# A layer norm's first half is moved from the openings of three attentions into the tails of the feed-forwards before them

## The chip, the cores and the metric

One NeuronCore of a Trainium2 chip runs the whole program in one launch. The metric is the device time of an execution in microseconds. A core has five engines that run their own instruction queues in order and meet by semaphores: TensorE (PE in the profile), VectorE (DVE), ScalarE (ACT), GpSimd (POOL) and SyncE (SP), which here only issues transfers.

## The reference

Four layers, each an attention and a feed-forward, on x of 8 batches x 100 tokens x 512 features, in float32. The context has 8 x 361 tokens.

```python
x = x + _L0_xattn_ref(_layernorm(x, axis=-1), ctx_2048, itok_BxS_0_1023, ...)
x = x + _L0_ffn_ref(_layernorm(x, axis=-1), ...)
x = x + _L1_xattn_ref(_layernorm(x, axis=-1), ctx_2048, mask_BxS2_ik0, ...)
x = x + _L1_ffn_ref(_layernorm(x, axis=-1), ...)
x = x + _L2_xattn_ref(_layernorm(x, axis=-1), ctx_2048, ...)
x = x + _L2_ffn_ref(_layernorm(x, axis=-1), ...)
x = x + _L3_xattn_ref(_layernorm(x, axis=-1), ctx_2048, ctx_2048, mask_BxS2_ff1, ...)
x = x + _L3_ffn_ref(_layernorm(x, axis=-1), ...)

def _layernorm(x, axis=-1, eps=1e-05):
    m = jnp.mean(x, axis=axis, keepdims=True)
    v = jnp.var(x, axis=axis, keepdims=True)
    return (x - m) / jnp.sqrt(v + eps)
```

Attentions 1, 2 and 3 project the normed x to queries and the context to keys and values, with 16 heads of 32. Feed-forward 0 adds to a shared network two of eight experts for each token; feed-forward 1 rounds activations and weights to few levels; feed-forward 2 is a gated network with 2048 inner features; feed-forward 3 sends each of 512 tokens to four of 16 experts.

## The kernel before, in words

**Layout.** The residual lies in SBUF feature-major: 128 partitions, KD = 4 tiles of features, T = 800 tokens in two halves of HALF = 400 (four batches of S = 100). float32 products are made of three products of rounded parts: a high part, copied by ScalarE, and a low part, what is left, subtracted by VectorE or GpSimd (`product`, L101 to L109).

**Stages.** Eight stages run one after the other: `l0x`, `l0f` (RoutedFfn), `l1x` (BoundedAttention), `l1f` (BitFfn), `l2x` (Attention), `l2f` (Ffn), `l3x` (LinearAttention), `l3f` (ChosenFfn). Each has a method for each engine, and the order of an engine's work is the order in which the code is written. Nothing is planned at run time. A stage ends when VectorE has made its last residual add and raises `residual_ready`; the next stage's GpSimd, SyncE and ScalarE work waits for it. VectorE and TensorE need no such wait for work on the first half of the tokens, because the adds of the first half are made first.

**The norm** (`Norm`) of a stage works by batches b of 100 tokens. `turn` transposes a batch on TensorE into a PSUM bank (16 transposes for four batches, L139). `stats` and `moments` on VectorE give mean and variance (L145, L151), `deviation` on ScalarE the square root (L156, which needs the table with Sqrt), `inverse` on VectorE the reciprocal and the shift (L162, L164), `normalise` on ScalarE the normed rows (L173), `back` on TensorE turns them back (L180), `high` on ScalarE (L186) and `low` on VectorE (L192) make the two parts. Deviation and inverse work on pairs of batches, so VectorE and ScalarE wait for each other twice in a half. The second half's turns use the banks of the first half, and each waits for the low part of the batch four earlier (`half_turn`).

**An opening** is what attentions 1, 2 and 3 do until their batches run (`Attention.pe`, `act`, `dve`, `pool`). ScalarE copies the high part of the context (L1810) and of twelve weight slabs (L1775), GpSimd subtracts the low parts (L1802, L1770), TensorE makes four key products (`pe_keys`), each of which needs one weight, then three value products (`pe_values`), which need eight weights, and then the query projection, which needs the norm and twelve weights. ScalarE copies the keys' high part (L1852), VectorE makes their low part (L1858). In the kernel before, the first half's statistics and normalising are in the opening, between the context copy and the weight copies, and the half turn of the second half stands between the second and the third key product. The slabs 6 to 11 are loaded into the buffers of slabs 0 to 5 when those are split.

**A tail** is a feed-forward's last product and its residual adds. The half turn of the next norm's first half already stands in the tails. In `l0f`, two expert sums come from DRAM in two transfers, one for each half (`sum_landed0`, `sum_landed1`); VectorE adds the two experts (`sums`, L1200), TensorE transposes them (`pe_sum`, L935), VectorE adds them to the residual (`add`, L1194). In `l1f` the last batch goes from the product (L2846) over ScalarE's copy (L2906) and four transposes (L2865) to the add (L2978). In `l2f` the last product is made in eight units of half the tokens, in four banks, each with an add (L683).

## Time and profile before

| | |
|---|---|
| Median of 3 runs | 2395.26 us (2393.09 to 2398.01) |
| Profiled execution | 2396.35 us, its span 2394.5 us |
| TensorE matmul busy | 2101.5 us, 88% |
| VectorE busy | 1086.1 us, 45% |
| ScalarE busy | 911.3 us, 38% |
| GpSimd busy | 495.7 us, 21% |
| Chain that ended last | TensorE 65%, DMA 11%, VectorE 10%, ScalarE 7%, issue 5% |

Times in the profile are microseconds from the start of the span. In the timeline a row is one instruction or several alike: start, duration, engine, line, operation, output and inputs; in brackets the idle time of its engine before it and what ended it. The granted clock is a share of TensorE's full clock of 2.4 GHz; 0.50 is 1.2 GHz. In the trace l1x opens at about 760 us, l2x at 1203 and l3x at 1776.

### The profile page before, as it was taken

The page shows a single profiled execution, that of the slowest core. Times are in us where ns is not written, and L with a number is a line of the kernel's source. Part 1 is how long each engine was busy: PE and PEld are TensorE (multiplying, and loading weights), DVE is VectorE, ACT ScalarE, POOL GpSimd, SP SyncE. Part 2 cuts the span into 40 slices and gives each one's busy share as a digit, 9 for nine tenths or more (in the row PEclk, how much of TensorE's full clock was granted, in tenths as well). Part 3 has the DMA queues.
Part 4 walks back from the last instruction along what each step waited for, and adds up shares of the span by engine and source line. Part 5 has one row for each costly group of instructions (what it writes and reads, how often), then busy time and mean ns, then how long its engine had stood idle before and what let it go on. Part 6 is the DMA issues. An engine that isn't in the chain of part 4 may idle for free.

```text
span 2394.5 us, 39229 instructions
## 1 busy us (share of the span) xinstructions
PE 2101.5 (88%) x14719; PEld 1693.1 (71%) x14719; DVE 1086.1 (45%) x2401; ACT 911.3 (38%) x1738; POOL 495.7 (21%) x358
## 2 busy tenths in 40 slices
PE   6989999896996888987978999889987999979997
PEld 5976666686445777775566777789986999945554
DVE  4447667565114255558825666422332555511111
ACT  3346556433222344455645454332233322222221
POOL 2233232232231211100031110033322111013322
PEclk7889999998997899978989999899999999989998
DMA  3110010127224121122020000021121100379995
GB/s 107 58 39 26 13 38 1 54 66 278 74 84 129 43 88 45 49 86 111 20 65 23 26 25 2 27 75 57 45 75 43 35 25 13 110 244 311 324 317 152
DMA packets 90860, 203.68 MB, mean 85 GB/s; under 512 B 9198, under 2 KB 14418, under 8 KB 88594
## 3 DMA queue, kind: packets, MB, share of 16 engines
q1 hardware_dynamic: 80562, 174.82, 22.4%
q0 software_dynamic: 10144, 26.75, 4.2%
q8 instruction: 104, 1.70, 0.3%
q14 instruction: 50, 0.41, 0.1%
HBM read 183.84 MB, written 19.53 MB: 85 GB/s over the span
## 4 chain that ended last, share of the span: by engine, by line
PE 65%; DMA 11%; DVE 10%; ACT 7%; issue 5%; POOL 1%; SPq 1%; ACTq 0%; DVEq 0%; POOLq 0%
PE psum L106 15%; PE psum L107 13%; PE psum L109 13%; DMA l3f_sum_dram<-l3f_y,l3f_rows 8%; PE psum L887 3%; PE psum L3376 2%; PE psum L2608 2%; PE psum L3346 2%; PE psum L2068 1%; PE psum L913 1%; PE psum L2273 1%; PE psum L1528 1%; DVE l2x_highest L2150 1%; PE psum L3362 1%; DVE ln_stats L145 1%
## 5 line engine op out<-in xcount | busy, mean ns | idle before, releaser
L1528 PE MATMUL psum<-l3f_gate_up,l3f_x_turned 128*128 128x352 f32 x496 | 154.2, 464 | 0.8 <-ACT l3f_x_turned L1587 0.8
L1528 PEld LDWEIGHTS psum<-l3f_gate_up,l3f_x_turned 128*128 128x128 f32 x496 | 93.0, 193 | 48.1 <-issue 1.7
L3135 POOL TENSOR_TENSOR l0x_w_lo<-l0x_w_raw,l0x_w_hi 128x512 fp32r<-128x512 f32 x52 | 71.8, 1398 | 152.0 <-ACT l0x_w_hi L3388 127.5
L2109 ACT ACTIVATE l2x_probs<-psum,l2x_shift 100x361 f32<-100x361 f32 x128 | 65.0, 559 | 98.2 <-DVE l2x_shift L2154 97.0
L3490 ACT ACTIVATE l0x_probs<-l0x_probs,l0x_lowest 100x361 f32<-100x361 f32 x128 | 75.1, 588 | 59.8 <-DVE l0x_lowest L3654 59.6
L106 PE MATMUL psum<-xn_hi,l2f_w_gu_hi 128*128 128x400 f32 x256 | 89.7, 350 | 8.8 <-ACT l2f_silu L588 4.9
L1802 POOL TENSOR_TENSOR l2x_ctx_lo<-l2x_ctx_raw,l2x_ctx_hi 128x1448 fp32r<-128x1448 f32 x8 | 26.3, 3289 | 339.8 <-ACT l2x_ctx_hi L1810 339.7
L107 PE MATMUL psum<-xn_lo,l2f_w_gu_hi 128*128 128x400 f32 x256 | 88.8, 347 | 0.0
L1503 POOL DMA_INDIRECT l3f_sum_dram<-l3f_y,l3f_rows x31 | 49.2, 1587 | 183.3 <-DMA l3f_sum_dram<-l3f_y,l3f_rows 143.6
L1554 PE MATMUL psum<-l3f_down,l3f_h_turned 128*128 128x512 f32 x186 | 85.1, 593 | 0.9 <-DVE l3f_h_turned L1619 0.9
L443 POOL TENSOR_TENSOR l2f_w_gu_lo<-l2f_raw_gu,l2f_w_gu_hi 128x512 fp32r<-128x512 f32 x32 | 43.0, 1353 | 203.6 <-ACT l2f_w_gu_hi L458 203.6
L1613 DVE TENSOR_TENSOR l3f_h<-l3f_silu,psum 128x352 f32<-128x352 f32 x31 | 16.2, 521 | 151.7 <-ACT l3f_silu L1600 120.4
L2302 ACT ACTIVATE ln_squares<-l1x_clipped,l1x_key_shift,l1x_key_scale 128x400 f32<-128x400 f32 (+1 forms) x96 | 62.3, 712 | 54.1 <-DVE l1x_clipped L2332 54.1
L887 PE MATMUL psum<-l0f_weights,l0f_x_turned 128*128 x160 | 75.2, 614 | 1.2 <-ACT l0f_x_turned L1029 0.8
L3376 PE MATMUL psum<-ln_squares,l0x_l_turned 128*128 128x400 f32 (+1 forms) x192 | 73.1, 516 | 0.9 <-ACT ln_squares L3499 0.9
L3654 DVE CUSTOM_DVE_ANT_0 l0x_probs<-psum,l0x_outside 100x361 f32<-100x361 f32 x128 | 62.6, 529 | 24.0 <-PE psum L3346 21.7
L641 DVE TENSOR_TENSOR l2f_h<-l2f_silu,psum 128x800 f32<-128x800 f32 x16 | 15.8, 988 | 125.7 <-PE psum L109 116.2
L3362 PEld LDWEIGHTS psum<-identity,l0x_probs 100*128 100x128 f32 (+1 forms) x384 | 38.0, 153 | 44.8 <-DVE l0x_probs L3665 20.3
L109 PE MATMUL psum<-xn_hi,l2f_w_gu_lo 128*128 128x400 f32 x256 | 69.3, 347 | 0.0
L2642 ACT ACTIVATE ln_squares<-psum 64x64 f32<-64x64 f32 x128 | 28.0, 218 | 105.9 <-PE psum L2608 103.5
L106 PE MATMUL psum<-l1x_w_hi,l1x_ctx_hi 128*128 128x512 f32 (+1 forms) x96 | 45.5, 474 | 25.5 <-DVE l1x_k_lo L1858 17.9
L3362 PE MATMUL psum<-identity,l0x_probs 100*128 100x100 f32 (+1 forms) x384 | 50.1, 265 | 19.9 <-DVE l0x_probs L3665 12.8
(533 smaller groups left out, 6181.1 us busy)
## 6 DMA issues: line engine op xcount, KB each, us to landing
l3f_gate_up<-in_slabs_dram SPq DMA_DIRECT2D x31, 1280.0 KB, 7.8
l3f_down<-in_slabs_dram SPq DMA_DIRECT2D x31, 512.0 KB
l0x_w_raw<-in_slabs_dram SPq DMA_DIRECT2D x52, 256.0 KB, 2.8
l0f_weights<-in_slabs_dram SPq DMA_DIRECT2D x8, 1536.0 KB
l1x_piece<-in_bit_w_dram SPq DMA_DIRECT2D x8, 1024.0 KB, 4.8
l1f_raw<-in_bit_w_dram SPq DMA_DIRECT2D x8, 1024.0 KB, 9.0
l2f_raw_gu<-in_slabs_dram SPq DMA_DIRECT2D x32, 256.0 KB, 2.6
l3f_down<-in_slabs_dram SPq DMA_DIRECT2D x31, 192.0 KB
```

Source lines behind the costliest of these rows:

```text
L106: pe.matmul(outs[i], weight_hi, moving[i][0], start=first, stop=False)
L107: pe.matmul(outs[i], weight_hi, moving[i][1], start=False, stop=False)
L109: mm = pe.matmul(outs[i], weight_lo, moving[i][0], start=False, stop=last)
L887: mm = pe.matmul(c.psum[:, t % 2, :], self.x_turned[:, t % 2, k, :], self.weights[:, bass.DynSlice(expert, 1), k * 512:(k + 1) * 512].rear ...
L1528: mm = pe.matmul(c.psum[:, bank + x, 0:self.INNER], self.x_turned[:, t % 2, k, :], self.gate_up[:, q, at:at + self.INNER], start=k == 0, s ...
L1554: mm = pe.matmul(c.psum[:, 6 + t % 2, :], self.h_turned[0:z - a, t % 2, k, :], self.down[0:z - a, q, k, :], start=k == 0, stop=k == 2)
L2109: act.activation(self.probs[:, m % 2, g, :], c.psum[0:S, g, 0:C], ACT.Exp, bias=self.shift[:, g:g + 1], scale=self.SCALE).then_inc(self.s( ...
L3135: pool.tensor_tensor(self.w_lo[:, place, :], self.w_raw[:, n % 3, :], self.w_hi[:, place, :], ALU.subtract).then_inc(self.s("w_split"), 1)
L3362: mm = pe.transpose(c.psum[0:z - a, 4 + t, g * S:(g + 1) * S], self.probs[:, g, a:z], c.identity[0:S, 0:S])
L3376: mm = pe.matmul(c.psum[:, 6, 0:4 * S], self.l_turned[0:z - a, q, t, :], turned[0:z - a, t, :], start=t == 0, stop=t == 2)
L3490: act.activation(self.probs[:, g, :], self.probs[:, g, :], ACT.Exp, bias=self.lowest[:, g:g + 1], scale=-1.0, accum_out=self.total[:, g:g ...
L3654: dve.tensor_tensor_reduce(self.probs[:, g, :], c.psum[0:S, g, 0:C], self.outside[:, q, :], -self.SCALE, 3.0e38, ALU.add, ALU.min, self.lo ...
```

## The change

In the tails of feed-forwards 0, 1 and 2, VectorE now also makes the first half's statistics, inverse and shift (`half_dve(..., 0)`), and ScalarE its deviation and normalised rows (`rows_ahead`, in `l1f` `half_rows`). In `l0f` the half turn moves from behind two of the second half's four sums to in front of them, and VectorE makes the first half's four adds and the statistics before it adds the experts of the second half. In `l2f` the half turn moves one unit forward and the statistics stand behind the fifth add. In `l1f` they stand in front of the last batch's add. The attentions open with the four turns back of the first half, then the turns of the second half, and then the key products; ScalarE makes the four high parts first, then weight copies and the second half's norm.

```diff
+def rows_ahead(n, act):
+
+    n.root_table(act)
+    half_rows(n, act, 0)
...
@@ ffn_pe, down: last product of l2f
-                if u == KD + 2:
+                if u == KD + 1:
                     pe.wait_ge(c.sem(st.name + "_added"), chunk * KD + KD)
                     half_turn(c.norms[st.index + 1], pe, 0)
@@ ffn_act
     ffn_schedule(act, st, gate_up, down)
+    rows_ahead(c.norms[st.index + 1], act)
@@ ffn_dve, down: adds of the last product
+                if u == KD:
+                    half_dve(c.norms[st.index + 1], dve, 0)
@@ RoutedFfn.pe
         for u in range(2 * KD):
-            if u == KD + 2:
+            if u == KD:
                 pe.wait_ge(self.s("added"), 3 * KD)
                 half_turn(c.norms[self.index + 1], pe, 0)
             self.pe_sum(c, pe, u)
@@ RoutedFfn.act
         out(self.TILES - 1)
+        rows_ahead(c.norms[self.index + 1], act)
@@ RoutedFfn.dve
         for u in range(KD):
             add(u, 2 * KD + u)
-            if u == 0:
-                sums(1)
+        half_dve(c.norms[self.index + 1], dve, 0)
+        sums(1)
         for u in range(KD, 2 * KD):
             add(u, 2 * KD + u)
@@ Attention.pe
-        n.back(pe, 0)
-        n.back(pe, 1)
-        self.pe_keys(pe, 0, 0, 0)
-        n.back(pe, 2)
-        n.back(pe, 3)
-        self.pe_keys(pe, 0, 0, 1)
+        half_back(n, pe, 0)
         pe.wait_ge(c.sem("residual_ready"), self.index + 1)
         half_turn(n, pe, 1)
-        self.pe_keys(pe, 0, 0, 2)
+        self.pe_keys(pe, 0, 0, 0)
+        self.pe_keys(pe, 0, 0, 1)
         n.back(pe, 4)
         n.back(pe, 5)
+        self.pe_keys(pe, 0, 0, 2)
         self.pe_keys(pe, 0, 0, 3)
         n.back(pe, 6)
         n.back(pe, 7)
@@ Attention.act
         self.split_context_high(act, 0, 0)
-        self.split_weight_high(act, 0)
-        n.deviation(act, 0)
-        n.normalise(act, 0)
-        n.normalise(act, 1)
-        n.deviation(act, 1)
-        self.split_weight_high(act, 1)
-        n.high(act, 0)
-        n.high(act, 1)
-        n.normalise(act, 2)
-        n.normalise(act, 3)
-        self.split_weight_high(act, 2)
-        n.high(act, 2)
-        n.high(act, 3)
+        for b in range(4):
+            n.high(act, b)
+        for i in range(2):
+            self.split_weight_high(act, i)
+        for g in (2, 3):
+            n.deviation(act, g)
+            n.normalise(act, 2 * g)
+            n.normalise(act, 2 * g + 1)
+            self.split_weight_high(act, g)
         act.wait_ge(self.s("vectors_landed"), 16)
         self.act_keys(act, 0, 0, 0)
-        self.split_weight_high(act, 3)
-        n.deviation(act, 2)
-        n.normalise(act, 4)
-        n.normalise(act, 5)
-        n.deviation(act, 3)
+        self.split_weight_high(act, 4)
         self.act_keys(act, 0, 0, 1)
         n.high(act, 4)
         n.high(act, 5)
-        n.normalise(act, 6)
-        n.normalise(act, 7)
-        self.split_weight_high(act, 4)
+        self.act_keys(act, 0, 0, 2)
         n.high(act, 6)
         n.high(act, 7)
-        self.act_keys(act, 0, 0, 2)
         self.act_keys(act, 0, 0, 3)
         for i in range(5, 12):
             self.split_weight_high(act, i)
@@ Attention.dve
-        half_dve(n, dve, 0)
         half_low(n, dve, 0)
+        half_dve(n, dve, 1)
...
         self.dve_keys(dve, 0, 0, 0)
-        half_dve(n, dve, 1)
         self.dve_keys(dve, 0, 0, 1)
-        half_low(n, dve, 1)
+        n.low(dve, 4)
+        n.low(dve, 5)
         self.dve_keys(dve, 0, 0, 2)
+        n.low(dve, 6)
+        n.low(dve, 7)
         self.dve_keys(dve, 0, 0, 3)
@@ BitFfn.act
         self.schedule(act, first, body)
+        half_rows(c.norms[self.index + 1], act, 0)
@@ BitFfn.dve
         self.schedule(dve, first, body)
+        half_dve(c.norms[self.index + 1], dve, 0)
         add(B - 1)
```

## Rows read from the trace of the kernel before

**Rows 1.** Timeline, opening of attention 1: start us, us, engine line
```profile
760.50 1.41 ACT L1810 ACTIVATE l1x_ctx_hi<-l1x_ctx_raw 128x1448 fp32r<-128x1448 f32 x1 [34.81 <-DVEq L1211]
...
762.06 3.23 POOL L1802 TENSOR_TENSOR l1x_ctx_lo<-l1x_ctx_raw,l1x_ctx_hi 128x1448 fp32r<-128x1448 f32 x1 [35.13 <-ACT l1x_ctx_hi L1810]
...
764.27 1.04 DVE L164 SCALAR_TENSOR_TENSOR ln_shift<-ln_moments,ln_inverse 100x2 f32<-100x2 f32 x1
...
771.40 0.90 ACT L186 ACTIVATE xn_hi<-psum 128x400 fp32r<-128x400 f32 x2 [1.14 <-PE psum L180]
...
771.94 1.06 DVE L192 TENSOR_TENSOR xn_lo<-psum,xn_hi 128x400 fp32r<-128x400 f32 x2 [2.88 <-ACT xn_hi L186]
...
773.55 1.91 PE L139 MATMUL psum<-identity,residual 128*100 128x128 f32 x16
...
774.19 1.29 DVE L145 BATCH_NORM_STATS2 ln_stats<-psum 100x6 f32<-100x512 f32 x2 [0.69 <-PE psum L139]
...
776.98 0.16 DVE L164 SCALAR_TENSOR_TENSOR ln_shift<-ln_moments,ln_inverse 100x2 f32<-100x2 f32 x1
...
777.26 1.45 ACT L173 ACTIVATE ln_squares<-psum,ln_shift,ln_inverse 100x512 f32<-100x512 f32 x2 [1.23 <-DVE ln_shift L164]
...
779.10 0.41 PE L106 MATMUL psum<-l1x_ctx_hi,l1x_w_hi 128*128 128x362 f32 x1
...
779.12 0.16 DVE L164 SCALAR_TENSOR_TENSOR ln_shift<-ln_moments,ln_inverse 100x2 f32<-100x2 f32 x1
...
781.17 0.92 PE L180 MATMUL psum<-identity,ln_squares 100*128 100x100 f32 x8
...
782.62 1.07 ACT L1852 ACTIVATE l1x_k_hi<-psum,l1x_vectors 128x362 fp32r<-128x362 f32 x2
...
783.51 3.29 ACT L1775 ACTIVATE l1x_w_hi<-l1x_w_raw 128x512 fp32r<-128x512 f32 x6
...
784.28 8.68 POOL L1770 TENSOR_TENSOR l1x_w_lo<-l1x_w_raw,l1x_w_hi 128x512 fp32r<-128x512 f32 x7 [0.95 <-ACT l1x_w_hi L1775]
...
788.15 0.77 PE L106 MATMUL psum<-l1x_w_hi,l1x_ctx_hi 128*128 128x512 f32 x1 [6.06 <-POOL l1x_w_lo L1770]
```

**Rows 2.** Timeline, openings of attentions 2 and 3: first context copy, first value product
```profile
1202.61 1.41 ACT L1810 ACTIVATE l2x_ctx_hi<-l2x_ctx_raw 128x1448 fp32r<-128x1448 f32 x1 [1.32 <-DVEq L2999]
...
1230.99 0.77 PE L106 MATMUL psum<-l2x_w_hi,l2x_ctx_hi 128*128 128x512 f32 x1 [6.05 <-POOL l2x_w_lo L1770]
...
1776.01 1.41 ACT L1810 ACTIVATE l3x_ctx_hi<-l3x_ctx_raw 128x1448 fp32r<-128x1448 f32 x1 [11.93 <-DVEq L697]
...
1804.41 0.77 PE L106 MATMUL psum<-l3x_w_hi,l3x_ctx_hi 128*128 128x512 f32 x1 [6.05 <-POOL l3x_w_lo L1770]
```

**Rows 3.** Timeline, tail of feed-forward 0
```profile
742.88 2.59 PE L935 MATMUL psum<-identity,l0f_weights 100*128 100x100 f32 x14 [0.48 <-DVE l0f_weights L1200]
...
743.51 0.57 DVE L1194 TENSOR_TENSOR residual<-residual,psum 128x400 f32<-128x400 f32 x1 [0.69 <-PE psum L935]
...
750.95 2.36 DVE L1200 TENSOR_TENSOR l0f_weights<-l0f_weights 100x1024 f32<-100x1024 f32 x2 [6.87 <-DMA l0f_weights<-l0f_y_dram]
...
754.81 3.65 PE L139 MATMUL psum<-identity,residual 128*100 128x128 f32 x16 [0.18 <-DVE residual L1194]
```

**Rows 4.** Stretch 766 to 774 us: busy us by engine; PEclk, DMA share, GB/s last
```profile
766.00:774.00 8.00, 7.74 (x45) 7.63 (x46) 2.94 (x7) 6.13 (x13) 3.72 (x4) 0.73 0.32 100
```

**Rows 5.** Timeline, tail of feed-forward 1
```profile
1200.61 0.69 ACT L2906 ACTIVATE l1f_out<-psum,l1f_h_step 100x512 f32<-100x512 f32 x1 [4.60 <-PE psum L2846]
...
1201.95 0.57 DVE L2978 TENSOR_TENSOR residual<-residual,psum 128x400 f32<-128x400 f32 x1 [5.97 <-PE psum L2865]
```

**Rows 6.** Timeline, tail of feed-forward 2
```profile
1771.22 1.91 PE L139 MATMUL psum<-identity,residual 128*100 128x128 f32 x16
...
1775.35 0.57 DVE L683 TENSOR_TENSOR residual<-residual,psum 128x400 f32<-128x400 f32 x1 [0.52 <-PE psum L109]
```

**Rows 7.** DMA issues from 724 to 800 us: KB each, median us to landing
```profile
l1x_w_raw<-in_slabs_dram SPq DMA_DIRECT2D x12, 256.0 KB, 8.1
```

## The prediction

> **What bounds the kernel now.** I read the chain of work that ended last first, then the timeline around the three places where a feed-forward hands over to an attention. In all three the same thing ends last. The attention's opening is a relay: ScalarE makes the high part of the context (L1810), norms and weights follow, TensorE makes the four key products, and then it stands idle for 6.06 us until GpSimd has split the eighth weight (L1770), which the value products need [rows 1]. I measure an opening from A, the start of L1810, which starts right behind the residual's last add, to V, the start of the first value product. It takes 788.15 - 760.50 = 27.65 us in the first attention [rows 1], and 28.38 and 28.40 us in the others [rows 2]. After V the products run on, and the weights that the projection needs are split some 8 us ahead of it, so what moves V moves the end. The reader is to see that V hangs on a row of queues: the fifth to eighth weights go to GpSimd only behind ScalarE's last key copy, and this copy stands behind the last two norm turns (781.17) and their high parts [rows 1].
>
> **The openings: the new V.** The first half's statistics and normalising leave the opening. What is left, counted from A = 0 with the durations of [rows 1]:
> - Context copy 1.41, four high parts at 0.45 each: 3.2. Two weight copies at 0.55: 4.3.
> - VectorE's lows start at 2.0 behind the first high; four at 0.53 end at 4.1. TensorE's turns of the second half start behind the first low, at 2.6. The first is read long before 4.1 at either clock.
> - Statistics start at 4.15. From there to the end of the first shift it takes 777.14 - 774.19 = 2.95: 7.1. Two normalisings 1.45: 8.65. The third weight copy, 0.6: 9.25. Deviation, inverse and shift of the last pair ended 0.57 behind the normalising in front of them (778.71 to 779.28); behind a weight copy I take 0.7: 9.95.
> - Here a block: L164 (two small inputs in SBUF) normally takes 0.16, but 1.04 at 764.27, and it ended at 765.31, within 0.02 us of the end of GpSimd's 3.23 us split that had begun at 762.06 [rows 1]. The new shift falls on the third weight's split (9.3 to 10.6), so I end it at 10.65.
> - Two normalisings: 12.15; the fourth weight copy: 12.75; its split on GpSimd, 1.24 (8.68 for 7): 14.05. The fourth key product may start at 14.1.
> - TensorE itself: four turns at the lower clock, 3.65 as in [rows 3], end at 6.2. The granted clock rose inside the stretch after the first turns, with a mean of 0.73 over 8 us, so about 4.3 us of it at 1.2 GHz and the rest at 2.4 [rows 4]. So the first key product, 2.07 at full clock (779.10 to 781.17), costs some 0.7 more and ends at 9.0; the second 11.1, two norm turns 0.92: 12.0, the third 14.1. It meets the weight at the same time.
> - Fourth key product to 16.2, where the last two norm turns start. From there to V it took 788.15 - 781.17 = 6.98 in the kernel before, with two key copies in it (1.07); now the third key is copied earlier, so 6.5: V = 22.7.
> The gains are 27.65 - 22.7 = 4.95, 5.7 and 5.7: 16.35 us. The bounds: without the block and with TensorE at full clock from the turns on, it is free at 13.1 and the weight is there at 13.4, so V = 22.0 (-2.1 in all); with each queue a further 0.7 late, +2.1. The table load in the first and third opening moves to the tail, where ScalarE has nothing else to do, and costs nothing; if that cover were gone it would stand once before the tail's first deviation.
>
> The Trainium skill, "SBUF — State Buffer", section "Who interferes with whom", states that a VectorE instruction with two SBUF inputs and a GpSimd instruction that reads SBUF exclude each other, and that the second to issue fully blocks until the first ends. The row agrees (1.04 against 0.16 us). By that rule the sum holds the block, as above; without it V could be up to 0.7 us earlier in each opening, if TensorE is also ready. The low parts (L192) have one input in PSUM, and by the same rule they don't wait; 1.06 us for two beside a GpSimd split agrees.
>
> **The tails: what is added there.** Statistics, deviation, inverse, shift of the first half stand now in VectorE's queue in front of the last residual adds. Each pair makes VectorE wait for ScalarE, and queued behind that wait are the adds, for which the whole next stage waits.
> - Feed-forward 0. In the kernel before, TensorE's half turn (3.65) stands between the sums of the last two-expert transfer and A [rows 3]. Adds 1 to 3 stood behind that transfer (750.95); now they run beside TensorE's 14 transposes (742.88, 2.59), the last to 746.25, and the half turn runs in the DMA's wait, to 749.95. The statistics follow the turns; the fourth ends at 750.75, inverse 751.1, two normalisings to 752.65, deviation and second shift 753.25. So the sums start at 753.3, not at 750.95: 2.35 late. From their end to A it took 760.50 - 753.31 = 7.2, less the turn 3.54. A = 753.3 + 2.36 + 3.54 = 759.2: 1.3 us earlier. If the turns ran at full clock, the sums would start at 752.1: 2.5 earlier.
> - Feed-forward 1. ScalarE's last output copy ends at 1201.30 [rows 5]. Then deviation 0.3, inverse and shift 0.4, two normalisings 1.45, deviation and shift 0.7 (less overlap): second shift at 1204.15, the last add (0.57) behind it, end 1204.8 instead of 1202.5. ScalarE then still has two normalisings, 1204.3 to 1205.7, ahead of L1810. A moves from 1202.61 to 1205.65: 3.05 later. Here nothing covers the wait, since ScalarE is late itself.
> - Feed-forward 2. The half turn starts one unit (1.1) earlier, at 1770.1 instead of 1771.22 [rows 6]; the fifth add ends at 1770.9; the whole statistics sequence of two pairs takes 779.28 - 774.19 = 5.09 [rows 1]: 1776.0. Adds 5 to 7, 0.58 each, end at 1777.8, against 1775.92: 1.9 later, and A with them (it stood 0.09 behind that add, 1776.01). The products are done at the same time as before and wait in their banks.
> The four turns back of the first half are issued ahead of the residual wait and end about 2.4 us behind it at the low clock, before the third high part asks for them: no cost.
>
> **The sum.** -16.35 - 1.3 + 3.05 + 1.9 = -12.7 us. The profiled execution took 2396.35 us (span 2394.5 and 1.85 around it), 1.09 above the median of 2395.26; it would become 2383.65, and the median 2382.6. No transfer is added or passed on another queue.
>
> **Rivals.**
> - A, the slabs come late. V needs the weights 6 and 7, whose transfers are issued when weights 0 and 1 are split (A + 6.1 and 7.4). The median landing in this stretch is 8.1 us [rows 7], so 15.5, and ScalarE asks at 18 to 19. It speaks against this rival; from a landing of 11.5 us on it sets V. If it took the 15.6 us that eat up 4.2 an opening, the time stays at about 2395. A gate of another kind that leaves V at A + 26 to 27 belongs here too. Chance 0.08.
> - B, the tails cost more: the handshakes of two engines in three queues each 2 us longer than counted (the sums in feed-forward 0 then start at 755.3). Time 2388.6. Chance 0.09.
> - C, the tails cost nothing, because the adds or the turns overlap more than the queues say: -16.35 alone gives about 2379, with the full-clock bound 2377. Chance 0.07.
> - D, slower: TensorE stays at 1.2 GHz through the key products. The openings' turns now stand apart from the products, with waits on each low part. At the low clock a turn takes 3.65 against 1.91 [rows 1, 3], a factor 1.9: products of 3.9 and norm turns of 1.75 put the fourth key product at 6.2 + 3 x 3.9 + 1.75 = 19.7, the last norm turns at 23.6 and V at 30.9, 2.5 to 3.3 later than before. With the tails' 3.65 that is +12, 2407. It decides from 4.2 us per opening on. Against it: the clock rose here after some 4.3 us with the same sparse work in front [rows 4], and the products that follow are as dense. Chance 0.05.
>
> **How the numbers follow.** The forecast holds 0.71: 2382.6, its own range 2379 to 2387 from the bounds above (openings -2.1 and +2.1, tails -1.2 and +1.5, and 1 us of scatter). A 0.08, B 0.09, C 0.07, D 0.05. The range to 2378 and 2389 takes in B and most of C, and leaves A and D out. No change means within 0.2%, 4.8 us, about what a measurement of this kernel can tell. Faster: forecast, B, C: 0.87. Same: A, 0.08. Slower: D, 0.05.
>
> **What would show it.** In the profile of the changed kernel: the idle of TensorE before the first value product still stands at 5 to 6 us, but V - A is 22 to 23.5 in all three; a shift of about 0.8 to 1 us ending with a GpSimd split, at A + 10; the half turn of feed-forward 0 between 746 and 750; its sums not at the DMA's landing but 2 us behind; the last add of feed-forward 1 behind a second shift, with two normalisings behind it. The forecast is wrong if V - A stays above 25, if a table load shows between the last deviation and the context copy, or if an add waits for ScalarE more than 5 us.

## The result and the profile after

The changed kernel took 2381.39 us (median of 4 runs, 2380.65 to 2383.91) against 2394.77 us for the kernel before (4 runs, 2393.09 to 2398.01). The ratio is 0.9942, with a 95% interval of 0.9927 to 0.9958: 13.4 us faster, where 12.7 was forecast. A second series gave 2380.40 us (median of 6 runs) against 2395.01 (e1 below).

A and V are again the starts of ScalarE's first context copy (now L1820) and of the first value product. The timeline of the changed kernel, opening of attention 1, answers to [rows 1]; the first column is the start, the second the duration:

```profile
757.50 1.41 ACT L1820 ACTIVATE l1x_ctx_hi<-l1x_ctx_raw 128x1448 fp32r<-128x1448 f32 x1 [4.05 <-DVEq L1221]
...
760.05 3.62 PE L139 MATMUL psum<-identity,residual 128*100 128x128 f32 x16 [0.59 <-DVE xn_lo L192]
...
766.97 1.29 POOL L1780 TENSOR_TENSOR l1x_w_lo<-l1x_w_raw,l1x_w_hi 128x512 fp32r<-128x512 f32 x1 [2.18 <-ACT l1x_w_hi L1785]
767.31 0.97 DVE L164 SCALAR_TENSOR_TENSOR ln_shift<-ln_moments,ln_inverse 100x2 f32<-100x2 f32 x1
...
771.79 0.43 PE L106 MATMUL psum<-l1x_ctx_hi,l1x_w_hi 128*128 128x362 f32 x1 [1.15 <-POOL l1x_w_lo L1780]
...
773.88 0.85 PE L180 MATMUL psum<-identity,ln_squares 100*128 100x100 f32 x8
...
775.21 0.57 ACT L1862 ACTIVATE l1x_k_hi<-psum,l1x_vectors 128x362 fp32r<-128x362 f32 x1
775.66 3.23 ACT L1785 ACTIVATE l1x_w_hi<-l1x_w_raw 128x512 fp32r<-128x512 f32 x6
776.38 4.95 POOL L1780 TENSOR_TENSOR l1x_w_lo<-l1x_w_raw,l1x_w_hi 128x512 fp32r<-128x512 f32 x4 [3.39 <-ACT l1x_w_hi L1785]
780.24 0.77 PE L106 MATMUL psum<-l1x_w_hi,l1x_ctx_hi 128*128 128x512 f32 x1 [5.50 <-POOL l1x_w_lo L1780]
```

The last row is V. TensorE still stands idle in front of it (5.50 us, 6.06 before), and it still waits for GpSimd's split of the eighth weight, but V - A is 22.74. The other two openings answer to [rows 2]:

```profile
1199.06 1.41 ACT L1820 ACTIVATE l2x_ctx_hi<-l2x_ctx_raw 128x1448 fp32r<-128x1448 f32 x1
...
1221.81 0.76 PE L106 MATMUL psum<-l2x_w_hi,l2x_ctx_hi 128*128 128x512 f32 x1 [5.50 <-POOL l2x_w_lo L1780]
...
1769.98 1.41 ACT L1820 ACTIVATE l3x_ctx_hi<-l3x_ctx_raw 128x1448 fp32r<-128x1448 f32 x1
...
1792.71 0.77 PE L106 MATMUL psum<-l3x_w_hi,l3x_ctx_hi 128*128 128x512 f32 x1 [5.50 <-POOL l3x_w_lo L1780]
```

That is 22.75 and 22.73. The three gains are 4.91, 5.63 and 5.67, together 16.21 us (16.35 forecast).

The timeline of the changed kernel in the tail of feed-forward 0, for [rows 3]:

```profile
739.41 2.36 DVE L1210 TENSOR_TENSOR l0f_weights<-l0f_weights 100x1024 f32<-100x1024 f32 x2 [7.19 <-DMA l0f_weights<-l0f_y_dram]
...
745.08 3.65 PE L139 MATMUL psum<-identity,residual 128*100 128x128 f32 x16 [0.66 <-DVE residual L1204]
...
751.72 0.16 DVE L164 SCALAR_TENSOR_TENSOR ln_shift<-ln_moments,ln_inverse 100x2 f32<-100x2 f32 x1
751.79 2.35 DVE L1210 TENSOR_TENSOR l0f_weights<-l0f_weights 100x1024 f32<-100x1024 f32 x2
```

The last sums stand right behind the second shift and no longer wait for the DMA. From the first sums to A it takes 757.50 - 739.41 = 18.09 us, against 760.50 - 740.47 = 20.03 before: 1.94 less.

The tail of feed-forward 1, for [rows 5]:

```profile
1194.19 0.69 ACT L2904 ACTIVATE l1f_out<-psum,l1f_h_step 100x512 f32<-100x512 f32 x1 [4.60 <-PE psum L2844]
1194.78 0.28 ACT L156 ACTIVATE ln_std<-ln_moments,eps 100x2 f32<-100x2 f32 x1
...
1197.52 0.56 DVE L2977 TENSOR_TENSOR residual<-residual,psum 128x400 f32<-128x400 f32 x1
1197.72 1.45 ACT L173 ACTIVATE ln_squares<-psum,ln_shift,ln_inverse 100x512 f32<-100x512 f32 x2 [0.51 <-DVE ln_shift L164]
```

A (1199.06) stands 4.87 us behind the start of the output copy, against 2.00 before: 2.87 more. And the tail of feed-forward 2, for [rows 6], with ScalarE's table load at its head:

```profile
1756.63 1.28 ACT L201 ACT_TABLE_LOAD   x1
...
1758.57 0.57 DVE L690 TENSOR_TENSOR residual<-residual,psum 128x400 f32<-128x400 f32 x1 [1.59 <-PE psum L109]
...
1768.36 1.52 DVE L690 TENSOR_TENSOR residual<-residual,psum 128x400 f32<-128x400 f32 x3
1768.57 1.45 ACT L173 ACTIVATE ln_squares<-psum,ln_shift,ln_inverse 100x512 f32<-100x512 f32 x2 [0.51 <-DVE ln_shift L164]
```

From the first unit's add to A it takes 1769.98 - 1758.57 = 11.41 us, against 9.99: 1.42 more. The table load and the small instruction behind it are followed by 6.8 us of idle time on ScalarE.

The account of the two spans (2394.5 and 2382.1, -12.4): openings -16.21; tails -1.94, +2.87 and +1.42; ahead of the first tail -1.06; the three stretches behind V +1.49, +1.73 and -0.70. So the openings and tails gave -13.86, where -12.7 was forecast, and the rest +1.46, where nothing was.

### The profile page after: what moved, and what is told of

The parts are those of the page before. It is cut to its first block, busy times and chain, and to the rows that moved or that the text cites. A ratio compares the mean times of both kernels' runs of the same rounds, so it can differ in the third digit from the quotient of the medians.

```text
span 2382.1 us, 39231 instructions
## 1 busy us (share of the span) xinstructions
PE 2103.5 (88%) x14719; PEld 1692.8 (71%) x14719; DVE 1085.5 (46%) x2401; ACT 912.1 (38%) x1740; POOL 496.0 (21%) x358
## 4 chain that ended last, share of the span: by engine, by line
PE 65%; DMA 11%; DVE 10%; ACT 7%; issue 5%; POOL 1%; ACTq 0%; SPq 0%; DVEq 0%; POOLq 0%
PE psum L106 15%; PE psum L107 13%; PE psum L109 13%; DMA l3f_sum_dram<-l3f_y,l3f_rows 9%; PE psum L896 3%; PE psum L3376 2%; PE psum L2606 2%; PE psum L3346 2%; PE psum L2066 2%; PE psum L922 1%; PE psum L2271 1%; DVE l2x_highest L2148 1%; PE psum L3362 1%; PE psum L2621 1%; DVE ln_stats L145 1%
## 5 line engine op out<-in xcount | busy, mean ns | idle before, releaser
L106 PE MATMUL psum<-l1x_w_hi,l1x_ctx_hi 128*128 128x512 f32 (+1 forms) x96 | 46.2, 481 | 25.1 <-DVE l1x_k_lo L1868 18.1
L3362 PE MATMUL psum<-identity,l0x_probs 100*128 100x100 f32 (+1 forms) x384 | 50.1, 265 | 19.9 <-DVE l0x_probs L3665 12.8
```

What stands on the lines that cost most here:

```text
L106: pe.matmul(outs[i], weight_hi, moving[i][0], start=first, stop=False)
L3362: mm = pe.transpose(c.psum[0:z - a, 4 + t, g * S:(g + 1) * S], self.probs[:, g, a:z], c.identity[0:S, 0:S])
```

## The experiments

All runs stand beside runs of the kernel before on the same chip, at 2394.2 to 2395.0 us in the median, and each ratio below is to these, with its 95% interval. Each kernel is the changed kernel with the edit shown. One table for all: V - A of the three openings; "path", the sum of the stretches that the change touches (first sums to A, output copy to A, first unit's add to A, and three times from A to VectorE's first value add, here W, which reads the first value product); the path against the changed kernel's; the median; and the median against 2381.39. The last column compares medians of different series, and the runs of one kernel lie 3 to 12 us apart, so one or two microseconds in it show nothing. The path is read from one profiled execution of each kernel.

| kernel | V - A | path | path, difference | median us | difference |
|---|---|---|---|---|---|
| before | 27.65, 28.38, 28.40 | 131.26 | +12.9 | 2394.77 | +13.4 |
| changed | 22.74, 22.75, 22.73 | 118.41 | 0 | 2381.39 | 0 |
| e1 | 22.74, 22.76, 22.74 | 118.23 | -0.2 | 2380.40 | -1.0 |
| e2 | 19.35, 19.37, 19.34 | 103.10 | -15.3 | 2364.89 | -16.5 |
| e3 | 21.45, 22.30, 21.44 | 113.84 | -4.6 | 2376.78 | -4.6 |
| e4 | 22.73, 22.72, 23.00 | 117.23 | -1.2 | 2382.66 | +1.3 |
| e5 | 22.74, 22.75, 22.74 | 120.37 | +2.0 | 2384.84 | +3.5 |
| e6 | 22.74, 22.70, 22.74 | 123.00 | +4.6 | 2384.80 | +3.4 |
| e7 | 29.73, 29.72, 29.74 | 136.37 | +18.0 | 2398.77 | +17.4 |
| e8 | 18.07, 18.64, 18.04 | 99.65 | -18.8 | 2361.29 | -20.1 |
| e9 | 22.73, 22.73, 22.72 | 115.43 | -3.0 | 2377.94 | -3.5 |
| e10 | 18.05, 18.07, 18.49 | 95.68 | -22.7 | 2359.26 | -22.1 |
| e11 | 16.41, 16.41, 16.41 | 88.99 | -29.4 | 2356.28 | -25.1 |

**e1, the changed kernel again, unedited.**

> The changed kernel itself once more, to see what repeats. If the working by queues holds, V - A (start of the context copy to the first value product) repeats at 22.7 us in all three openings, and the time is 12.5 to 13.5 us below the kernel before. The stretches between the openings, which the change does not touch, differed by +1.5, +1.7 and -0.7 us between the two profiles: if that is scatter of the clock's phase, they come out otherwise here, by 1 us or so either way; if the change costs something there, +1.5 and +1.7 repeat.

Ratio 0.995, interval 0.9934 to 0.9966: 14.6 us below the kernel before (12.5 to 13.5 expected). V - A and the tails repeat within 0.03 us, A to W within 0.2. The first stretch behind V took 410.17 us, not 413.95, at a higher granted clock (PEclk, third from the end; the changed kernel, then e1):

```profile
780.24:1194.19 413.95, 357.66 (x4062) 284.80 (x4062) 244.90 (x570) 206.99 (x306) 33.10 (x15) 0.89 0.17 62
778.95:1189.10 410.15, 353.52 (x4062) 281.64 (x4062) 245.05 (x570) 206.92 (x306) 33.10 (x15) 0.90 0.17 63
```

The other two did not come out otherwise: 536.73 and 589.40 us, against 536.76 and 589.39 in the changed kernel and 535.03 and 590.11 before. By the test set above, the first stretch's +1.49 was scatter, while the second's +1.7 speaks for a cost of the change there; 0.85 of it is the first value product alone (5.50 us against 4.65 before). But in e5, whose openings are the same, this product took 4.35 and the stretch 533.52, so the cause stays open.

**e2, is V set by when ScalarE hands over the weights?**

```
         self.act_keys(act, 0, 0, 1)
+        self.split_weight_high(act, 5)
         n.high(act, 4)
         n.high(act, 5)
+        self.split_weight_high(act, 6)
         self.act_keys(act, 0, 0, 2)
+        self.split_weight_high(act, 7)
...
-        for i in range(5, 12):
+        for i in range(8, 12):
```

> ScalarE copies weights 5, 6 and 7 between the key copies and the high parts, no longer behind the last key copy. Theory (V hangs on ScalarE's and GpSimd's queues): GpSimd works through the weights 3 to 7 with hardly a gap, the eighth is split at A + 19.3 instead of 22.7, so V - A is 19.4 in each opening, 3.4 less; TensorE idles 2 us instead of 5.5, and if it then keeps its full clock, the first value product group costs up to 2 us less. In all 10 to 16 us below the changed kernel: 2365 to 2371. Rival (the transfers of slabs 6 and 7 set V): V - A stays at 22.7, time within 2 us of the changed kernel, and ScalarE waits on the transfer in front of the seventh copy.

Ratio 0.9874 (0.9859 to 0.9888), V - A 3.4 us less in each opening. Timeline of this kernel (its A is 758.04), and then the windows (engine busy times, PEclk third from the end) from V to W, of the changed kernel and of this one, in opening 2:

```profile
771.00 11.20 POOL L1780 TENSOR_TENSOR l1x_w_lo<-l1x_w_raw,l1x_w_hi 128x512 fp32r<-128x512 f32 x9 [2.20 <-ACT l1x_w_hi L1785]
...
777.39 0.76 PE L106 MATMUL psum<-l1x_w_hi,l1x_ctx_hi 128*128 128x512 f32 x1 [2.12 <-POOL l1x_w_lo L1780]
```

```profile
1221.81:1227.30 5.49, 5.46 (x12) 3.77 (x12) 0.00 (x0) 2.04 (x2) 5.41 (x5) 0.50 0.51 197
```

```profile
1211.73:1214.80 3.07, 3.04 (x12) 2.14 (x12) 0.00 (x0) 1.62 (x4) 3.07 (x3) 1.00 0.99 388
```

GpSimd now splits nine weights in a row from A + 12.96; the fifth of them is the eighth weight, and 12.96 + 5 x 1.24 = 19.2 is V. So from that split on GpSimd alone sets V. And the gain is larger than 3 x 3.4 = 10.2, because in openings 2 and 3 the first value product itself became shorter: in opening 2 5.49 us at a granted clock of 0.50 in the changed kernel, behind 5.50 us of idle, and 3.07 at 1.00 here, behind about 2 us. The prediction had counted only to V. The sum to W holds it (5.2 us in all). In opening 1 nearly nothing of this came, though the idle time in front was the same 2.12 us:

```profile
777.39:781.94 4.55, 4.50 (x12) 3.25 (x12) 0.01 (x1) 2.58 (x4) 4.55 (x4) 0.65 0.68 264
```

**e3, the shift out of the way of the third split.**

```
-        for g in (2, 3):
-            n.deviation(act, g)
-            n.normalise(act, 2 * g)
-            n.normalise(act, 2 * g + 1)
-            self.split_weight_high(act, g)
+        n.deviation(act, 2)
+        n.normalise(act, 4)
+        n.normalise(act, 5)
+        n.deviation(act, 3)
+        self.split_weight_high(act, 2)
+        n.normalise(act, 6)
+        n.normalise(act, 7)
+        self.split_weight_high(act, 3)
```

> The last pair's deviation is taken ahead of the third weight's copy, so its shift runs before GpSimd splits that weight. Theory (the shift is blocked by the split it overlaps): the shift takes 0.16 instead of 0.97 us, the fourth weight is split 1.3 us earlier, and V - A is 1.15 less where TensorE waited for it (openings 1 and 3 in the profile) and 0 in opening 2, where TensorE was busy: 2.3 us faster in all, 2379. Rival (0.97 is the operation's own time there, and nothing is blocked): the shift still takes 0.97, the weight comes 0.5 earlier, 1 us in all.

Ratio 0.9936 (0.9922 to 0.9949); V - A 1.29, 0.45 and 1.29 less. Timeline of this kernel:

```profile
765.48 0.16 DVE L164 SCALAR_TENSOR_TENSOR ln_shift<-ln_moments,ln_inverse 100x2 f32<-100x2 f32 x1
...
765.84 1.28 POOL L1780 TENSOR_TENSOR l1x_w_lo<-l1x_w_raw,l1x_w_hi 128x512 fp32r<-128x512 f32 x1 [2.36 <-ACT l1x_w_hi L1785]
```

The same instruction takes 0.16 us ahead of the split and 0.97 beside it. The shift ends at A + 9.45 instead of 10.78, and 0.81 of these 1.33 us is the block; the other 0.52 comes from the deviation's place ahead of the weight copy. Opening 2 was to gain nothing, because TensorE is busy there, and gained 0.45: its clock stood at 0.50 until A + 8.4, and the fourth key product began at A + 13.96, behind TensorE's own work, against 13.08 in opening 1. The expectation was 2.3 us in all; the path is 4.6 shorter, of which 3.0 lie in V - A, 1.3 in the first value products and 0.3 in the first tail.

**e4, feed-forward 0: sums ahead of the second inverse.**

```
         sums(1)
+        then.inverse(dve, 1)
```

(The rest of the first half's work stands in front of the sums as before.)

> In feed-forward 0 VectorE adds the experts of the second half before it makes the second pair's inverse and shift, so it no longer waits for ScalarE's normalising with the landed transfer behind it. Theory (this handshake holds the sums back by 1.9 us): from the first sums to A it takes 16.2 us instead of 18.1, time 1.9 below the changed kernel, 2379.5. Rival (the transfer lands only then): no change of A, and VectorE idle in front of the sums, released by the DMA.

The sums start again at the landing, 11.04 us behind the first sums instead of 12.38, and A comes 1.34 earlier (16.75), not the 1.9 expected, because VectorE now waits for the transfer:

```profile
749.51 2.36 DVE L1210 TENSOR_TENSOR l0f_weights<-l0f_weights 100x1024 f32<-100x1024 f32 x2 [0.56 <-DMA l0f_weights<-l0f_y_dram]
```

The median (ratio 0.9947, 0.9934 to 0.996) doesn't show so little; the stretch does.

**e5, feed-forward 1: the add ahead of the statistics.**

```
-        half_dve(c.norms[self.index + 1], dve, 0)
         add(B - 1)
+        half_dve(c.norms[self.index + 1], dve, 0)
```

> The changed kernel, but in the tail of feed-forward 1 VectorE makes the last residual add first and the first half's statistics, inverses and shifts behind it. It asks which queue sets A in this tail. Theory (ScalarE's: the context copy stands behind four normalisings, and these hang on VectorE's shifts): the add can start 1.34 us behind the output copy's start and ends at 1.9, so the first inverse starts at 1.9 instead of 0.9 and all behind it is 1.0 later: A stands 5.9 us behind the output copy instead of 4.87, and the time is 2382, 1 us above the changed kernel's. Rival (the last add sets A, as the prediction's working on feed-forward 2 has it): A stands 2.0 to 2.9 us behind the copy, and the time is 2378 to 2379.

The rival falls, and the expected number too: output copy (1190.61) to A is 8.37 us, not 5.9. Timeline of this kernel:

```profile
1191.95 0.57 DVE L2977 TENSOR_TENSOR residual<-residual,psum 128x400 f32<-128x400 f32 x1 [5.97 <-PE psum L2863]
1192.44 1.29 DVE L145 BATCH_NORM_STATS2 ln_stats<-psum 100x6 f32<-100x512 f32 x2
...
1198.98 1.41 ACT L1820 ACTIVATE l2x_ctx_hi<-l2x_ctx_raw 128x1448 fp32r<-128x1448 f32 x1
```

The residual is complete at 1192.5, and A comes 6.5 later. In this kernel VectorE raises the residual's signal only behind the statistics, so the distance alone doesn't tell which queue sets A; the changed kernel does. There the last add ends at 1198.08, and A comes 0.98 later without idle time behind ScalarE's last normalising. The expectation had counted only the inverses as moved behind the add; the edit moves the statistics too, which had run under the last products and now wait through 5.97 us for the add. Ratio 0.9958 (0.9942 to 0.9974).

**e6, feed-forward 0: the half turn back behind the DMA's wait.**

```
-            if u == KD:
+            if u == KD + 2:
...
-        half_dve(c.norms[self.index + 1], dve, 0)
-        sums(1)
+            if u == 0:
+                sums(1)
         for u in range(KD, 2 * KD):
             add(u, 2 * KD + u)
+            if u == KD + 1:
+                half_dve(c.norms[self.index + 1], dve, 0)
```

> The changed kernel, but in the tail of feed-forward 0 TensorE's half turn goes back behind the sixth sum and the statistics behind the sixth add, so that the sums of the last two-expert transfer again start at its landing; deviation, inverse, shift and normalising stay in the tail. It asks what the tail's earlier turn is worth. Theory (the turn in the DMA's wait pays for the pairs that VectorE now waits for): the stretch from the first sums to A is the 20.03 us of before plus about 2.3 for the statistics, the two pairs' turns between VectorE and ScalarE and the last adds behind them, so 22.3 against 18.09, and the time is about 4.3 us above the changed kernel's 2381: 2385. Rival (the last adds and the pairs overlap, so that the place of the turn doesn't matter): 18 to 19 us, and 2381 to 2382.

First sums to A is 22.64 us, 4.55 more; the time is 3.4 more (ratio 0.9958, 0.9943 to 0.9973). The half turn starts behind the sixth add, at 753.71, not inside the wait:

```profile
753.71 3.65 PE L139 MATMUL psum<-identity,residual 128*100 128x128 f32 x16 [0.18 <-DVE residual L1204]
```

So without the earlier turn this tail would have cost 2.6 us instead of giving 1.9.

**e7, the new order without the move.** The tails are those of the kernel before; in the opening:

```
         self.split_context_high(act, 0, 0)
+        half_rows(n, act, 0)
...
+        half_dve(n, dve, 0)
         half_low(n, dve, 0)
```

> The changed kernel's new order of the attention's opening (turns, then key products), but with no work in the tails: all three tails are those of before, and the statistics, deviations and normalisings of the first half stand at the head of the opening, behind the context copy. It tells the order's part from the move's. Theory (the openings are short because the first half's relay is gone, and the order only spends that): the relay of two pairs takes 5.1 to 6 us and lies again in front of the first high part, so V - A is 28.5 to 30 in all three; with 2.4 us less in the tails than in the changed kernel the time is 2396 to 2401, no better than before. Rival (the order alone brings the gain, because the weights are copied earlier): V - A is 23 to 26 and the time 2380 to 2390.

Ratio 1.0021 (1.0012 to 1.003): the order alone is some 4.6 us slower than the kernel before (2394.18 in this series). The timeline of its first opening:

```profile
759.97 1.28 ACT L156 ACT_TABLE_LOAD   x1
...
760.10 3.23 POOL L1808 TENSOR_TENSOR l1x_ctx_lo<-l1x_ctx_raw,l1x_ctx_hi 128x1448 fp32r<-128x1448 f32 x1 [36.11 <-ACT l1x_ctx_hi L1816]
...
761.79 1.56 DVE L164 SCALAR_TENSOR_TENSOR ln_shift<-ln_moments,ln_inverse 100x2 f32<-100x2 f32 x1
```

The relay's first shift is held up by the context's split and ends with it, at 763.35 and 763.33. V - A is 29.73, 29.72 and 29.74; the table load in the first lies under that split and adds nothing.

**e8, the three orders of e2, e3 and e4 together.**

> The changed kernel with three orders tried singly: weights 6 to 8 copied by ScalarE between the key copies, the last deviation ahead of the third weight copy, and in feed-forward 0 the last sums ahead of the second inverse and shift. Theory (what ends last in front of the value products is now GpSimd, which splits nine weights without a pause from A + 12.96 on, and value products need the fifth of them; the shift's order lets the fourth split start at A + 11.64 instead): V is 11.64 + 5 x 1.244 = 17.9, so V - A about 18.0 against 19.35 with the weights alone, 4 us less in three openings; the first sums to A take 16.75; time 2365 - 4 - 1.3 = 2359.5. Rival (TensorE's key products or the landing of the weights' transfers set V from here on): V - A stays at 19 or more, and the time is 2362 or more.

Ratio 0.9872 (0.9858 to 0.9886). The timeline, with A at 755.71:

```profile
767.37 11.21 POOL L1788 TENSOR_TENSOR l1x_w_lo<-l1x_w_raw,l1x_w_hi 128x512 fp32r<-128x512 f32 x9 [0.69 <-ACT l1x_w_hi L1793]
...
773.78 0.47 PE L106 MATMUL psum<-l1x_w_hi,l1x_ctx_hi 128*128 128x512 f32 x1 [2.11 <-POOL l1x_w_lo L1788]
```

11.66 + 5 x 1.245 = 17.9, and V follows at 18.07: GpSimd sets V, as expected, in openings 1 and 3. In opening 2 (18.64) the rival holds in part. TensorE's clock stood at 0.50 until A + 8.4, the fourth key product began at A + 13.95 instead of 13.12, and what ended last was VectorE's low part of the fourth key:

```profile
1208.77 0.80 PE L106 MATMUL psum<-l2x_w_hi,l2x_ctx_hi 128*128 128x512 f32 x1 [1.84 <-DVE l2x_k_lo L1876]
```

**e9, feed-forward 1: the first pair ahead of the output copy.**

```
+            if not now:
+                then.deviation(act, 0)
+                then.normalise(act, 0)
+                then.normalise(act, 1)
+                then.deviation(act, 1)
             if before:
...
-        half_rows(c.norms[self.index + 1], act, 0)
+        then.normalise(act, 2)
+        then.normalise(act, 3)
```

> The changed kernel, but in the tail of feed-forward 1 ScalarE makes the first deviation, the first pair of normalisings and the second deviation ahead of its last output copy, not behind it. Theory (the tail of feed-forward 1 costs 2.9 us because ScalarE takes up the first deviation only behind the output copy, although its statistics were there 3.8 us earlier and ScalarE stood idle for 4.6 us): the output copy starts 0.25 later at most, A stands about 2.1 us behind it instead of 4.87, so A is 2.5 us earlier, counted from TensorE's half turn of this tail (7.8 instead of 10.27), and the time is 2378.4. Rival (VectorE's last add or the landing of the products is what ends last): A moves by less than 1 us, and the time is 2380 to 2381.

Ratio 0.9938 (0.9925 to 0.9951). Timeline of this kernel:

```profile
1188.77 0.29 ACT L156 ACTIVATE ln_std<-ln_moments,eps 100x2 f32<-100x2 f32 x1 [1.43 <-DVE ln_moments L151]
...
1191.94 0.69 ACT L2911 ACTIVATE l1f_out<-psum,l1f_h_step 100x512 f32<-100x512 f32 x1
...
1193.94 1.41 ACT L1820 ACTIVATE l2x_ctx_hi<-l2x_ctx_raw 128x1448 fp32r<-128x1448 f32 x1
```

The copy to A is 2.00 us again, as in the kernel before, and the copy itself starts no later: from TensorE's half turn of this tail to A it is 7.40 us, against 10.28 in the changed kernel. So the whole cost of this tail, 2.87 us, was the place of four instructions in ScalarE's queue.

**e10, all four orders.**

> The three orders of the combined kernel, and the first pair of rows ahead of the last output copy in feed-forward 1. Theory (the parts lie in different stretches and add up): V - A about 18.1, 18.6 and 18.0, A 2.0 us behind the output copy in feed-forward 1, 16.7 us from the first sums to A; the time is the combined kernel's 2361.3 less 2.6 to 2.9: 2358.5. Rival (the time saved in one place is lost again behind it, as a later start of the second attention's weights): 2361 or more.

Ratio 0.9841 (0.9823 to 0.9858). The parts add up within 1 us: the path is 22.7 us shorter, against 18.8 for e8 and 3.0 for e9. The opening at 18.5 is here the third, again one whose clock was low into the first key products (to A + 8.1).

**e11, e10 with every weight early and the last key ahead of the last high parts.**

```
         n.deviation(act, 2)
+        self.split_weight_high(act, 2)
+        self.split_weight_high(act, 3)
         n.normalise(act, 4)
         n.normalise(act, 5)
         n.deviation(act, 3)
+        self.split_weight_high(act, 4)
...
         self.act_keys(act, 0, 0, 2)
+        self.act_keys(act, 0, 0, 3)
         n.high(act, 6)
         n.high(act, 7)
```

(Weights 5 to 7, counted from 0, follow behind key copies 0, 1 and high part 5; VectorE's low part of the last key moves in the same way.)

> The kernel with all four orders, and in the opening also: ScalarE copies the third and fourth weight behind the first two and the fifth behind the last deviation, so that GpSimd splits without a pause from the context's split on; and the last key product is copied ahead of the last two high parts. Theory (in the combined kernel V waits for two things that end together at A + 17.8, GpSimd's split of the eighth weight and VectorE's low part of the last key; TensorE itself is done at A + 16.0; GpSimd with 8 splits of 1.25 from A + 4.8 is done at 14.8): TensorE sets V, V - A is 16.3 to 16.9, and the time is some 4.5 us below the kernel with the four orders: about 2354. Rival (GpSimd without a pause holds up each shift until its split ends, up to 1.25 us each, as a two-input instruction of VectorE was held up before; or the slabs of the seventh and eighth weight land too late): the last pair of rows and with it the last norm turns come later, V - A stays at 17.5 or more, the time at 2357 or more.

Timeline of this kernel (A at 758.29), and the window from V to W:

```profile
763.08 6.25 POOL L1788 TENSOR_TENSOR l1x_w_lo<-l1x_w_raw,l1x_w_hi 128x512 fp32r<-128x512 f32 x5
...
767.59 0.52 DVE L164 SCALAR_TENSOR_TENSOR ln_shift<-ln_moments,ln_inverse 100x2 f32<-100x2 f32 x1
...
774.70 0.50 PE L106 MATMUL psum<-l1x_w_hi,l1x_ctx_hi 128*128 128x512 f32 x1 [0.60 <-DVE l1x_k_lo L1876]
```

```profile
774.70:777.80 3.10, 3.06 (x12) 2.17 (x12) 0.91 (x3) 2.98 (x6) 2.39 (x2) 1.00 0.90 341
```

V - A is 16.41 in all three. TensorE's idle in front of V is down from 5.50 to 0.60, and VectorE's low part of a key, which follows TensorE's last key product, releases it, no longer GpSimd. The shifts are still held up (0.52 ends at 768.11, with a split at 768.08), but those waits are covered by the key products. The time is 2356.28 us (2354 expected), ratio 0.9837 (0.9821 to 0.9854). Its path is 6.7 us shorter than e10's, the medians differ by 3.0, and the intervals overlap: what became of the rest is open.

## Why the prediction was right

- **Openings, right.** V hangs on the queues of ScalarE and GpSimd. e2 shows it by moving three weight copies and nothing else (V - A 3.4 less), and e8 by putting V where GpSimd's queue, counted out, has it in two openings; e7 shows that the relay of the first half (7.0 us of V - A) is what the move takes out, and that the new order without it is slower.
- **Inside the opening, one step mis-sized without effect.** I had TensorE and the fourth weight meet at 14.1. The weight came at 771.79, A + 14.29. In openings 1 and 3 TensorE had already been idle for 1.15, since 13.14, the bound I gave for the full clock. I had charged the first key product 0.7 us of low clock. In opening 1 the clock rose with the first key product, at 763.7; in opening 2 it stayed at 0.50 until A + 8.4, this product took 3.07 us instead of 2.07, and TensorE and the weight met as counted. The windows of the changed kernel, two of opening 1 and one of opening 2 (PEclk third from the end):

```profile
757.50:763.70 6.20, 5.60 (x29) 4.87 (x27) 4.17 (x9) 4.32 (x8) 4.63 (x3) 0.50 0.20 49
763.70:774.70 11.00, 9.85 (x64) 9.35 (x64) 5.00 (x12) 7.06 (x14) 4.90 (x4) 1.00 0.39 103
...
1205.25:1207.45 2.20, 2.20 (x7) 2.20 (x8) 1.19 (x5) 0.98 (x2) 1.08 (x1) 0.50 0.44 113
```

- **The block, right.** The shift that was to end at A + 10.65 ended at 768.28, A + 10.78, within 0.02 us of the third split's end (768.26). The Trainium skill, "SBUF — State Buffer", section "Who interferes with whom", has VectorE instructions with two inputs in SBUF and GpSimd's reads of SBUF exclude each other. By that rule all these shifts agree: 0.97, 0.52 and 1.56 us beside a split, 0.16 without. e3, which takes the shift out of the way, gave 0.45 to 1.29 us an opening, of which the block is at most 0.81. For the low parts (L192), which were not to wait, the prediction's row at 771.94 shows nothing, since no split runs beside it. This pair of the kernel before does, with the same 1.06 us:

```profile
767.66 1.28 POOL L1770 TENSOR_TENSOR l1x_w_lo<-l1x_w_raw,l1x_w_hi 128x512 fp32r<-128x512 f32 x1 [1.15 <-ACT l1x_w_hi L1775]
768.00 1.06 DVE L192 TENSOR_TENSOR xn_lo<-psum,xn_hi 128x400 fp32r<-128x400 f32 x2 [0.55 <-ACT xn_hi L186]
```

- **Feed-forward 0, -1.94 against -1.3.** The mis-sized term is the statistics sequence. I had the sums at 753.3, 12.8 us behind the first sums, and they stood 12.38 behind; the rest of the 0.6 lies in the adds behind them. e6 shows that the earlier turn pays for it; e4 that the second pair's handshake costs 1.3 here.
- **Feed-forward 1, +2.87 against +3.05.** The mechanism holds: A follows ScalarE's last normalising, 0.98 us behind the add. But the prediction took "nothing covers the wait, since ScalarE is late itself" as given by the change. ScalarE had stood idle for 4.60 us in front of the output copy, with the first pair's statistics done; e9 takes the whole term away.
- **Feed-forward 2, +1.42 against +1.9.** The sequence of two pairs took 5.08 us (1763.36 to 1768.44), as counted. The mis-sized term is the last three adds: they took 1.52 us together beside waiting products and ended 1.44 behind the second shift, not 1.8. A stands 0.09 behind the last add, as in the kernel before; ScalarE's last normalising, which ends at 1770.02, would have let it go hardly earlier.
- **Table load, no cost, right.** It lies in front of 6.8 us of idle time in feed-forward 2 and of 23.0 us in feed-forward 0; e7 adds that it was hidden in the opening as well.
- **Rival A.** I held a landing of 8.1 us against the 11.5 that would hurt [rows 7]. That row mixes in slabs that are asked for long before. The DMA issues of the opening alone, with the median time to landing last; the line is the same for the changed kernel (757 to 790 us) and for the kernel before (760 to 800 us):

```profile
l1x_w_raw<-in_slabs_dram SPq DMA_DIRECT2D x6, 256.0 KB, 2.6
```

The rival was much further off than I said, and e11, which asks for the slabs earliest, shows no wait for one in front of V.
- **Rival D.** It fell. The clock was at 1.00 during the key products in openings 1 and 3; in opening 2 only the first ran at 0.50, and V - A was 22.75 all the same. Where it did matter I had not looked: from V to W.
- **B and C** are out by the stretches: the tails cost 2.35 us in sum (3.65 forecast), neither the 9.65 of B nor 0.

The total came out 0.7 us apart, but this is partly luck. The openings and tails gave 1.2 us more than forecast, and the stretches behind V, which I had unchanged, took 2.5 us back (+1.49, +1.73 and -0.70). Only the first of these moved between two profiles of the changed kernel; the other two repeated in e1, and no experiment shows why.

## What to carry to other kernels

When an engine waits at a stage's head, write the relay out as queues and ask for the first instruction that stands behind work it doesn't need; moving three weight copies gained 16 us where moving a whole norm half had gained 13. Before work goes into a tail, look where its helper engine idles there, and place it into that gap and not behind the tail's last instruction. Carry the sum one step past the wait that you remove, since the clock of what follows can change with the idle time in front of it; here it did so in some openings and not in others.

## What the runs showed of the hardware

- The first value product, the same 12 matmuls each time, took 3.05 to 3.12 us at a granted clock of 1.00 and 4.25 to 5.50 us at 0.68 to 0.50. All 27 that stood behind 5.5 to 6.1 us of idle TensorE had the low values. Of the nine behind 1.8 to 2.1 us (e2, e8, e10), five ran at 1.00 and four at 0.63 to 0.67; the three behind 0.6 us (e11) ran at 1.00. So the full clock goes with a shorter idle time in front, but 2 us of it are no warrant. The Trainium skill, "TensorE: Matmul & The Clock Gate", Part 1, states that the clock gate knows two levels only, half and full; by that rule a mean such as 0.63 is a mix of both within the stretch. The trace agrees: in the changed kernel's opening 1, at a mean of 0.59, the matmuls start 0.43 us apart until 784.21 and about 0.23 apart from there on.
- Two profiles of the changed kernel differ by 3.8 us in the 414 us behind V of opening 1, at granted clocks of 0.89 and 0.90 (e1). In the stretch behind V of opening 2 the kernels differ too: its first 53 us had a clock of 0.85 in the changed kernel and in e1, and the whole stretch took 536.8 and 536.7 us; with 0.94 in e2 it took 532.9, with 0.91 in e3 534.8. Whether an edit brings one or the other there was not settled.
- A GpSimd split of a weight took 1.25 to 1.32 us in every run, alone or beside VectorE. In the openings it was always VectorE's small shift that waited, and it ended within 0.03 us of the end of the GpSimd instruction under way.
